# One GpSimd product of 1024 columns per unit of the state scan, with re-written engine orders and banks

## The reference, cut to what matters

```
h = exp(dt[..., None] * A) * h + (x_c * dt)[..., None] * B_t[:, None, :]   # scan over 512 tokens
y = einsum('bn,bdn->bd', C_t, h)                                          # sum over N = 16 states
```

## Time and profile before

| | us |
|---|---|
| median of 3 runs (lowest, highest) | 5944.29 (5938.65, 5945.28) |
| the profiled execution | 5941.06 |
| its span | 5938.9 |
| TensorE matmuls busy in the span | 5262.0 (89%) |
| VectorE busy | 5103.3 (86%) |
| GpSimd busy | 4194.8 (71%) |
| ScalarE busy | 4094.7 (69%) |
| granted TensorE clock, mean | 0.96 |

### The profile page before, as it was taken

One profiled execution on the slowest core, in us unless ns is written; L12 is line 12 of the kernel. 1 busy time (PEld: TensorE's weight loads), 2 busy tenths in 40 slices (PEclk: granted clock), 3 DMA queues, 4 the chain that ended last, 5 costly groups with the idle time before them and its releaser, 6 DMA issues. The chain is left out here.

```text
span 5938.9 us, 115651 instructions
## 1 busy us (share of the span) xinstructions
PE 5262.0 (89%) x32280; PEld 3518.1 (59%) x32280; DVE 5103.3 (86%) x7776; ACT 4094.7 (69%) x6407; POOL 4194.8 (71%) x2545
## 2 busy tenths in 40 slices
...
GB/s 129 132 140 142 140 148 149 142 128 142 135 152 147 129 142 128 144 152 135 143 126 140 144 151 143 127 141 133 152 148 126 142 133 143 151 142 137 142 129 39
DMA packets 521726, 814.74 MB, mean 137 GB/s; under 512 B 80432, under 2 KB 227288, under 8 KB 520976
## 3 DMA queue, kind: packets, MB, share of 16 engines
...
## 5 line engine op out<-in xcount | busy, mean ns | idle before, releaser
L584 POOL TENSOR_TENSOR state<-scan_in,bc 128x1024 f32<-128x1024 f32 x1024 | 2405.9, 2362 | 650.6 <-PE pY L940 504.2
L1201 DVE TENSOR_TENSOR_SCAN pD<-pD,state 128x512 f32<-128x512 f32 x1536 | 1851.2, 1216 | 190.1 <-ACT pD L708 119.9
L708 ACT ACTIVATE pD<-scan_in,A 128x512 f32<-128x512 f32 x2048 | 1397.5, 690 | 656.5 <-DVE state L1209 572.6
L940 PE MATMUL pY<-ident,state 128*128 128x128 f32 x8192 | 1214.0, 282 | 102.9 <-DVE state L1209 94.8
L940 PEld LDWEIGHTS pY<-ident,state 128*128 128x128 f32 x8192 | 928.6, 145 | 335.7 <-DVE state L1209 145.8
L1209 DVE TENSOR_TENSOR state<-pD,bc 128x512 f32<-128x512 f32 x1536 | 1024.6, 680 | 44.7 <-issue 24.6
L1259 DVE TENSOR_REDUCE mx<-pM 128x1 f32<-128x512 f32 (+3 forms) x1408 | 850.3, 630 | 69.8 <-PE pM L1030 67.5
L809 ACT ACTIVATE region<-pM 128x512 f32<-128x512 f32 (+1 forms) x1408 | 733.6, 556 | 255.3 <-PE pM L1048 224.8
L571 POOL TENSOR_TENSOR state<-state,bc 128x512 f32<-128x512 f32 x512 | 644.2, 1273 | 342.9 <-DVE state L1201 333.4
L1201 DVE TENSOR_TENSOR_SCAN state<-pD,state 128x512 f32<-128x512 f32 x512 | 606.0, 1207 | 105.0 <-ACT pD L708 105.0
L1046 PE MATMUL pM<-region 98*128 98x512 bf16 (+3 forms) x2048 | 535.5, 310 | 101.5 <-DMA region<-mrow 45.0
...
## 6 DMA issues: line engine op xcount, KB each, us to landing
bc<-bc_d SPq DMA_DIRECT2D x2048, 256.0 KB, 4.0
region<-qk_d SPq DMA_DIRECT2D x640, 128.0 KB, 3.6
...
region<-qk_d SPq DMA_DIRECT2D x256, 64.0 KB, 3.0
...
```

The lines of the kernel that those rows point to most:

```text
L584: nc.gpsimd.tensor_tensor(state[:, at_:at_ + JP], us[:, parity(b), k // N * JP:(k // N + 1) * JP, :], bc[:, k % BC_SLOTS, 0, :].unsqueeze( ...
L708: act.activation(pD[DECAY_BANK[e]][:], dts[:, parity(b), j], ACT.Exp, scale=A[:, j, n:n + 1]).then_inc(a_ok.sem, 1)
L940: ins = pe.matmul(y_part(t, e % JP), state[:, e % RING, t * P:(t + 1) * P], ident[:], is_transpose=True, start=False, stop=(e % PASS >= PA ...
L1201: v.tensor_tensor_scan(h if e in POOL_C else decay, decay, h, 0.0, ALU.mult, ALU.add)\
```

## The change

`times_c` multiplies both blocks of a unit at once: it takes the unit's number, waits for both scans, reads C's row through a broadcast over the two blocks, and counts both on the semaphore. The step pc is now numbered by unit, and stands once where two stood. All five order texts and the bank numbers are written anew. The loop's branch now lies elsewhere: TensorE's between f1_6 and f1_7 (its text begins with -f1_7), ScalarE's between st3_3_0 and dec62, VectorE's between c13 and l0s, GpSimd's between pc7 and f1_0, SP's between put and rc22. The diff, cut: of the orders, GpSimd's whole and of the others the lines that are spoken of below; SP's order and the bank numbers (`PLACE`) are left out.

```diff
-            def times_c(b, e):
-
-                slot = state[:, e % RING]
-                b.wait(pool, s_ok, e + 1)
-                b.wait(pool, *row_in(b, e // JP, 1))
-                nc.gpsimd.tensor_tensor(slot, slot, bc[:, e // JP % BC_SLOTS, 1, :], ALU.mult).then_inc(pp_ok.sem, 1)
+            def times_c(b, k):
+
+                e = k * JP
+                slots = state[:, e % RING:e % RING + JP]
+                b.wait(pool, s_ok, e + JP)
+                b.wait(pool, *row_in(b, k, 1))
+                nc.gpsimd.tensor_tensor(slots, slots, bc[:, k % BC_SLOTS, 1, :].unsqueeze(1).broadcast_to([P, JP, L]),
+                                        ALU.mult).then_inc(pp_ok.sem, JP)
...
     "POOL": """
-        fill8 fill9 pc14 -f1_0 pc15 +l0s fill10 +l0a fill11 +l0b +l0c +l1s fill12 pc22 pc23 fill13 -x2 -x2b -l3s
-        +ql0 fill14 -xb +ql1 fill15 +ql2 fill16 pc30 pc31 fill17 +ql3 -gb fill18 -put fill19 fill20 fill21 pc38
-        pc39 fill22 fill23 fill24 fill25 fill26 pc46 pc47 fill27 fill28 pc54 pc55 fill29 fill30 fill31 +u0 +u1
-        +fill0 pc62 pc63 +fill1 +fill2 +fill3 +fill4 +pc6 +pc7 +fill5 +fill6 l2s +fill7
+        -f1_0 +l0s fill10 +l0a +l0b fill11 +l0c +l1s fill12 fill13 pc11 -x2 -x2b fill14 -l3s +ql0 fill15 -xb +ql1
+        +ql2 fill16 pc15 fill17 +ql3 -gb fill18 -put fill19 fill20 fill21 pc19 fill22 fill23 fill24 fill25 pc23
+        fill26 fill27 fill28 fill29 pc27 fill30 fill31 +u0 +u1 +fill0 pc31 +fill1 +fill2 +fill3 +fill4 +fill5
+        +pc3 +fill6 l2s +fill7 +fill8 +fill9 +pc7
     """,
     "ACT": """
-        z0 dec5 dec6 dec7 dec8 dec9 dec10 dec11 z1 dec12 dec13 -l2a dec14 -h2t0 -h2t1 dec15 z2 dec16 dec17 -f1_0
-        -f1_1 dec18 -f1_2 -f1_3 dec19 -f1_4 dec20 +l0a -f1_5 dec21 -f1_6 -f1_7 dec22 -gelu mt0 dec23 dec24 z3
-        dec25 +l1a zsilu dec26 dec27 st0_0_0 +xt0 +xt1 st0_0_1 dec28 st0_0_2 +qk0 dec29 st0_0_3 st0_1_0 st0_1_1
...
-        dec56 oe2 dec57 st3_0_0 st3_0_1 st3_0_2 dec58 st3_0_3 st3_1_0 dec59 +sp2 st3_1_1 st3_1_2 st3_1_3 dec60
-        st3_2_0 st3_2_2 dec61 st3_3_0 dec62 oe3 dec63 +dec0 +v0 +dec1 +ud ot0 +dec2 ot1 +dec3 yt0 +v1 +dec4 yt1
-        yt2 yt3
+        -dec62 -dec63 -oe3 v0 dec0 dec1 ud v1 -ot0 dec2 dec3 -ot1 -yt0 -yt1 dec4 -yt2 -yt3 dec5 z0 dec6 dec7 dec8
+        dec9 dec10 dec11 z1 dec12 dec13 -l2a -h2t0 -h2t1 z2 dec14 dec15 dec16 -f1_0 dec17 -f1_1 -f1_2 -f1_3 dec18
+        dec19 -f1_4 +l0a -f1_5 dec20 -f1_6 dec21 -f1_7 -gelu dec22 dec23 z3 dec24 mt0 +l1a dec25 zsilu dec26 +xt0
...
+        st3_0_1 st3_0_2 st3_0_3 st3_1_0 dec58 dec59 +sp2 st3_1_1 dec60 st3_1_2 st3_1_3 dec61 st3_2_0 st3_2_2
+        st3_3_0
     """,
     "PE": """
-        z3 mt0 add19 -f2_0 +xt0 -f2_1 mx1_0 add20 +xt1 st0_0_0 mx1_1 add21 add22 st0_0_1 st0_0_2 +qk0 st0_0_3
-        add23 st0_1_0 add24 add25 st0_1_1 mx1_2 mx1_3 +qk1 st0_1_2 -h3t0 -h3t1 +qk2 -route st0_1_3 +xs0 +xs1 +qk3
-        st0_2_0 pv0_0 pv0_1 st0_2_2 -lora add26 st0_3_0 add27 -axt mx1_4 mx1_5 -out0 mx1_6 -out1 mx1_7 mx1_8
...
-        +add10 +add11 +z2 h2t0 h2t1 +add12 +add13 f1_0 f1_1 f1_2 f1_3 f1_4 +mx0_4 f1_5 f1_6 f1_7 +add14 +mx0_5
-        +mx0_6 +mx0_7 +add15 +mx0_8 +add16 +mx0_9 +add17 +mx0_10 +add18
+        -f1_7 mx0_6 add14 mx0_7 add15 mx0_8 mx0_9 add16 add17 mx0_10 z3 add18 mt0 add19 -f2_0 +xt0 -f2_1 st0_0_0
+        mx1_0 st0_0_1 +xt1 add20 add21 mx1_1 st0_0_2 st0_0_3 add22 st0_1_0 st0_1_1 +qk0 add23 add24 st0_1_2 add25
+        add26 mx1_2 add27 mx1_3 +qk1 -h3t0 -h3t1 +qk2 st0_1_3 -route +xs0 +qk3 +xs1 pv0_0 st0_2_0 st0_2_2 pv0_1
...
+        +add4 sso1 +add5 +z1 +add6 +add7 +mx0_2 +add8 +z2 +add9 +add10 +add11 h2t0 h2t1 +add12 +mx0_3 +add13 f1_0
+        f1_1 f1_2 f1_3 f1_4 f1_5 +mx0_4 +mx0_5 f1_6
     """,
     "DVE": """
-        c16 c17 +l0s scan18 c18 scan19 mx0_4 c19 scan20 c20 scan21 c21 mx0_5 mx0_6 mx0_7 mx0_8 mx0_9 mx0_10
-        scan22 +l1s scan23 scan24 mt0 scan25 c24 c25 -f2_0 scan26 -f2_1 c26 mx1_0 mx1_1 scan27 c27 -l3s +qk0
-        mx1_2 mx1_3 +qk1 scan28 c28 scan29 c29 +qk2 -route +xs0 scan30 +qk3 +xs1 -lora scan31 scan32 mx1_4 mx1_5
...
+        +l0s scan14 scan15 mx0_3 scan16 c16 scan17 c17 scan18 scan19 c18 mx0_4 c19 mx0_5 scan20 mx0_6 mx0_7 mx0_8
+        mx0_9 scan21 mx0_10 c20 +l1s c21 scan22 mt0 scan23 scan24 -f2_0 scan25 c24 c25 scan26 -f2_1 scan27 c26
+        c27 mx1_0 mx1_1 -l3s +qk0 scan28 scan29 mx1_2 c28 mx1_3 +qk1 c29 scan30 +qk2 -route +xs0 +qk3 +xs1 -lora
```

More of the change, by code:

```diff
@@ L1364 @@
     "SP": """
[L1365 to L1368, removed]
+        -rc22 -rb24 -rb25 -rc21 -x1p -rb22 -ld3 -rc23 -rb23 -mt2 -rc26 -rb26 -rc24 -rb29 -rb28 -rc25 -rb27 xp ld0
@@ L1369 @@
+        -rc28 -rb31 -rc27 -rb30 -rc29 -mt3 -rc30 rb0 rc0 rb1 -rc31 rb2 +load rc2 rc1 rb3 rb4 ld2 rb6 rb5 rc4 rb8
+        rc3 rc5 rb7 rb9 rc6 -xr rc7 rc9 rb10 rc8 rc10 rc12 rb11 rc11 rb12 rb14 ld1 rb13 rc13 rb15 rc14 mt0 rc16
+        rb16 rb17 rc15 rc17 +qk0 rc18 +qk1 +l1a rb18 rb19 rc20 rb21 mt1 rb20 rc19 +qk2 +qk3 -put
     """,
     "POOL": """
-        fill8 fill9 pc14 -f1_0 pc15 +l0s fill10 +l0a fill11 +l0b +l0c +l1s fill12 pc22 pc23 fill13 -x2 -x2b -l3s
-        +ql0 fill14 -xb +ql1 fill15 +ql2 fill16 pc30 pc31 fill17 +ql3 -gb fill18 -put fill19 fill20 fill21 pc38
@@ L1417 @@
+        c52 mx3_10 scan53 mt3 c53 scan54 scan55 scan56 scan57 c56 c57 scan58 scan59 +mx0_0 on2 c58 +mx0_1 c59
+        +sp3 scan60 c60 scan61 c61 scan62 scan63 on3 +scan0 +scan1 +c0 +c1 gate1 +scan2 +scan3 +c2 +c3 +scan4 +c4
+        +scan5 +c5 +scan6 +scan7 +scan8 +scan9 +c8 +c9 sso0 +scan10 +scan11 sso1 l2s +c10 +c11 +scan12 +scan13
+        +c12 +mx0_2 +c13
     """,
```

59 lines of the change are left out of this document (30 added, 29 removed).

## The result

The changed kernel takes **5954.3 us** in the median (5944.1 to 5960.8, 22 runs) against 5945.3 of the kernel before (22 runs on the same chips): ratio 1.0013, 95% interval 1.0007 to 1.0019. That is 0.13% slower, where I forecast 0.6% faster. The 5954 lies in my range and within the 0.2% that I called no change; the forecast direction is wrong. The profiled execution took 5954.47 us, 13.4 more than that of before.

What follows compares the result with a forecast made beforehand. Turns were taken as bounded alternately by TensorE and VectorE. From 5941 us, 13 (dec60), 10 (ScalarE's stop) and 13 (h3t0) came off, giving 5905; adding 3 gave 5908 us, range 5845 to 5985.

Steps and rivals of the forecast that it cites:

- TensorE's stop: Once-per-body stop of 4.51 us, moved from add18|z3 to f1_6|f1_7; taken as 0, with gelu's cover holding by 0.5 us.
- The relay: Each turn: A (f1_0 to behind out1, 67 us) goes at TensorE's pace, B (the rest, 112 us) at VectorE's.
- the stop ahead of gelu: Rival at f1_6|f1_7: the stop delays gelu and f2_0; 59 us on top of the sum, 5967 us; chance 0.18.
- rows 2: Profile table of two turns by stretch; TensorE worked 60.20 us, not 65.16, in the f1_0-to-out1 stretch with its stop.
- ScalarE's stop: Once-per-body stop of 2.8 us, moved from z0 to before dec62; 1.7 exposed instead of 2.59, 10 us gained.
- dec60: ScalarE before scan60: dec60 behind one eviction instead of three; 0.7 us a turn in 19 turns, 13 us gained.
- TensorE before h3t0: TensorE idles 0.64 us there until l3a; two more adds fill it; 0.4 us a turn, 13 us gained.
- The product: GpSimd's wide product saves 47 us of GpSimd work but counts 0 on the path; upper bound 35 us slower.
- The rival that charged 1.09 us at TensorE's adds: The wide product is waited for: each of 43 waits grows 1.09 us, 47 us, 5991 us without gains; chance 0.08.
- qk1: VectorE's 2.52 us wait, filled by scans 28, 29 and c28; 0 on the path, bound 81 us.
- The rest: Regrouped scans and products, SP's order, table loads taken as even; new bank numbers bounded at +-10 us.
- no change: Rival: each small gain in VectorE's stretch is swallowed by the next wait; 5932 to 5956 us; chance 0.20.

Runs made afterwards that it cites:

- e5: Kernel before with only TensorE's order text cut ahead of f1_7, so its stop moves there from ahead of z3: ratio 0.9873 to the kernel before.
- e13: Changed kernel with mx0_4 put in bank 3 instead of 1 and mx0_5 moved behind f1_7 (on VectorE behind scan20): ratio 0.9905 to the kernel before.
- e15: Changed kernel with TensorE's text cut two f1 steps earlier, at f1_4|f1_5: ratio 0.9901 to the kernel before.
- e6: Kernel before with only ScalarE's order text cut ahead of dec62 instead of ahead of z0: ratio 0.9943 to the kernel before.
- e9: Kernel before with both stops moved, TensorE's to f1_6|f1_7 and ScalarE's ahead of dec62, narrow product kept: 5839.4 us, ratio 0.9829 to the kernel before.
- e8: Changed kernel with ScalarE's stop put back ahead of z0: ratio 1.0002 to the kernel before.
- e16: e9 with dec60 alone moved ahead of the evictions st3_1_2 and st3_1_3 on ScalarE: ratio 0.9850 to the kernel before.
- e2: Changed kernel with the two products of 512 columns kept, back to back where the wide one stands: 5948.7 us, ratio 1.0006 to the kernel before.
- e1: Kernel before (old order, banks, stops) with only GpSimd's pairs of products merged into one of 1024 columns: 6007.6 us, ratio 1.0104 to the kernel before.
- e10: e1 with one swap on GpSimd, fill5 ahead of pc3: ratio 1.0055 to the kernel before.
- e11: e10 with one more swap, on TensorE, ot1 ahead of add62: ratio 1.0011 to the kernel before.
- e3: Changed kernel with dec58 moved back ahead of the evictions st3_0_3 and st3_1_0 on ScalarE: ratio 1.0017 to the kernel before.
- e17: e15 with dec58 and dec60 both back at their old places among ScalarE's evictions: ratio 0.9885 to the kernel before.

## Why the prediction was wrong, step by step

- **TensorE's stop: "I take 0".** This step failed, and it decides. The relay was right, but I gave the stop one length, 4.5 us, wherever it stands, and with "lower bound 0: the stop stays in A" I excluded a gain without asking what hides a stop. By itself the move is worth 75 us (e5). The stop falls from 5.2 us in the mean to 1.1, and the step behind it no longer runs slow in 12 of 13 turns: z3 had taken 3.56 us behind the stop against 1.88 without it. In the changed kernel the steps just ahead of the branch (mx0_4 in f1_4's bank, with mx0_5 and f1_6 behind it) take that back: 64 to 67 us return when that bank and mx0_5's place are changed (e13) or the cut is moved (e15). My rival, the stop ahead of gelu, did not come about as I told it: A did not grow, it shrank by 1.1 us where 5.5 were to be had (e5).
- **The table under both stops.** From rows 2 I read that the A with the stop lost 6.8 us of TensorE, and the two Bs stand there as equally long. By the marks of f1_0 and out1 that A is 8.7 us longer than its neighbour in the mean, and the B with ScalarE's stop 3.6 us, together 160 us in 13 bodies. I had priced the two stops at 4.51 and 2.59 us, 59 and 34 in all, so what moving them could give was too small from the start.
- **ScalarE's stop: 10 us.** The term was mis-sized: alone 34 us (e6), which was my outer bound. Only 0.6 us stays exposed in e9 (0.52 in the turn shown), not 1.7. In the changed kernel the cover is gone: scan62 waits 2.1 us in the mean, and the move back changes nothing that is clear of noise (e8). e16 shows dec60's move doing just that. I had priced the two moves as independent terms, and they share one slack.
- **dec60: 13 us.** The wait fell to 0.16 us as forecast, the time did not (e16): scan61 got 0.4 us of wait in every turn, and scan62 1.2 us more in the 13 turns with ScalarE's stop. Failed step: "of which I count 0.7 us a turn".
- **TensorE before h3t0: 13 us.** Not there: the undisturbed A is 69.21 us against 69.04.
- **The product: 0.** Right for the new order to within 4 us (e2). I had seen that fills move ahead of the product, but argued the price from one place, unit 15. The price was at units 3 and 31, 55 us together (e1, e10, e11). The rival that charged 1.09 us at TensorE's adds had half the mechanism: fills queued behind the product are the other half.
- **qk1: 0 on the path.** Right in effect: the undisturbed A kept its length.
- **"The rest, even"** and *no change* as the next wait swallowing each gain: e3 and e16 show it in B. But B without a stop is 1.0 us longer than before, so the rest was not even. The scans' waits for decays are shorter in sum but twice as many, before and after (us, times):

```profile
  ACT pD L708: 224.9, 121
...
  ACT pD L710: 200.5, 265
```

And the level total hides large parts: about 109 us lie between the changed kernel and e9 by the ratios (1.0013 and 0.9829), 113 between the two profiled executions. By the table of means some 50 of them are the A with TensorE's stop, 41 the B with ScalarE's, 12 the other B, and 9 the last turns. The experiments account for the first part (e13, e15) and for some 10 us of the second (e17); the product adds up to 4. Which adds, scans and banks cost the rest of B, I did not take apart. So the rival *no change* has the right number largely by luck: what cancelled was not only the small gains in B that it speaks of, but 75 us of TensorE's stop against the steps put ahead of it, which it does not mention.

The best kernel run is e9, the old order with nothing but the two stops moved: 0.9829, 1.8% faster than the changed kernel.
